# Counting a graph's edges tile by tile in the permuted order: one 128-column product per tile in place of three

## The reference, cut to what matters

```python
for l in range(6):                       # first network, h: [2500, 128]
    W = ssp(edge_attr @ mlp_w1[l] + mlp_b1[l]) @ mlp_w2[l] + mlp_b2[l]
    W = W * C[:, None]                   # cutoff of the edge's length
    msg = (h @ conv_w1[l])[src] * W
    agg = segment_sum(msg, dst)
    h = h + ssp(agg @ conv_w2[l] + conv_b2[l]) @ lin_w[l] + lin_b[l]
x = layernorm(x + h)
for l in range(3):                       # second network, h starts as x
    agg = segment_sum(h[src], dst)
    z = (1 + eps[l]) * h + agg
    h = relu(z @ W1[l] + b1[l]) @ W2[l] + b2[l]
x = layernorm(x + h)
```

## Time and profile before

| | us |
|---|---|
| median of 3 runs | 6492.66 (6480.39 to 6500.86) |
| the profiled execution | 6501.15 |
| its span, first to last instruction | 6499.5 |
| TensorE busy | 5331.1 (82% of the span) |
| GpSimd busy | 4028.7 (62%) |
| VectorE busy | 3774.4 (58%) |
| ScalarE busy | 2761.8 (42%) |
| mean granted TensorE clock | 0.913 of full speed |

### The profile page before, as it was taken

How to read it: one execution, slowest core, us unless ns; L and a number is a source line. 1 busy time by engine, 2 the same in 40 slices (tenths; PEclk the granted TensorE clock), 3 DMA queues, 4 the chain that set the end, 5 groups by cost and what they waited for, 6 DMA issues and landing times.

```text
span 6499.5 us, 130502 instructions
## 1 busy us (share of the span) xinstructions
PE 5331.1 (82%) x34529; PEld 4194.0 (65%) x34530; DVE 3774.4 (58%) x10468; ACT 2761.8 (42%) x4801; POOL 4028.7 (62%) x5030
## 2 busy tenths in 40 slices
PE   1043648999989989989999899998999889998989
PEld 0043637777767777767777677776777767777744
DVE  7321324666666666666666666666666666666632
ACT  0021314445445444445444444444454445444422
POOL 5777762666656666656666566665666656666600
PEclk5576879999999999999999999999999999999999
DMA  8265956333333333233333333333333333333300
GB/s 323 74 222 192 301 173 219 108 106 105 103 103 107 106 105 104 94 112 108 105 106 103 104 106 104 105 101 107 104 108 106 103 99 111 104 106 103 98 15 9
DMA packets 430774, 775.66 MB, mean 119 GB/s; under 512 B 55098, under 2 KB 115972, under 8 KB 427348
## 3 DMA queue, kind: packets, MB, share of 16 engines
q1 hardware_dynamic: 388108, 728.55, 35.0%
q0 software_dynamic: 20640, 34.39, 1.6%
q10 hardware_dynamic: 21928, 11.64, 0.6%
HBM read 605.57 MB, written 168.79 MB: 119 GB/s over the span
## 4 chain that ended last, share of the span: by engine, by line
PE 66%; POOL 9%; issue 9%; DVE 8%; DVEq 5%; DMA 2%; ACT 1%; SPq 1%; ACTq 0%; POOLq 0%
PE ps_a L709 16%; PE ps_h L795 13%; PE ps_a L689 13%; PE ps_w L699 12%; POOL permuted L574 9%; PE ps_pair L721 4%; DVE aggT L1460 3%; PE ps_pair L908 3%; DVE counts L1524 2%; DVEq L341 2%; PE ps_pair L723 1%; DVEq L336 1%; DVEq L430 1%; DVE hid L1599 1%; DMA hid<-permuted 0%
## 5 line engine op out<-in xcount | busy, mean ns | idle before, releaser
L592 POOL TENSOR_SCALAR phot<-pwin_now,prel_now,pcut_now 128x128 f32<-128x128 f32 x4224 | 3315.9, 800 | 1632.9 <-PE ps_a L709 1601.0
L1460 DVE TENSOR_TENSOR aggT<-aggT,ps_a 128x128 f32 x4224 | 1219.0, 289 | 1155.3 <-PE ps_a L709 598.2
L689 PEld LDWEIGHTS ps_a<-hi_mid,buffers 128*128 128x128 f32 x8448 | 1157.6, 199 | 573.0 <-issue 569.8
L1077 ACT ACTIVATE xc<-ps_h 128x512 f32<-128x512 f32 x1056 | 630.3, 597 | 2108.8 <-PE ps_h L795 2093.6
L709 PE MATMUL ps_a<-phot,ex_msg 128*128 128x128 f32 x8448 | 1267.4, 296 | 184.0 <-DVE aggT L1460 183.8
L709 PEld LDWEIGHTS ps_a<-phot,ex_msg 128*128 128x128 f32 x8448 | 1082.8, 201 | 229.8 <-issue 120.5
L795 PE MATMUL ps_h<-buffers,edge_w 112*128 112x512 f32 x2112 | 1181.2, 643 | 11.1 <-DVE hid L1599 9.7
L689 PE MATMUL ps_a<-hi_mid,buffers 128*128 x8448 | 1162.4, 282 | 3.5 <-DMA hi_mid<-node_table 3.5
L699 PE MATMUL ps_w<-edge_w,hid 128*128 128x128 f32 x8448 | 1121.1, 276 | 1.3 <-ACT ps_w L1041 1.1
L1599 DVE SCALAR_TENSOR_TENSOR hid<-xc,ps_h 128x512 f32<-128x512 f32 x1056 | 724.2, 686 | 539.8 <-PE ps_w L699 508.4
L699 PEld LDWEIGHTS ps_w<-edge_w,hid 128*128 128x128 f32 x8448 | 1035.1, 193 | 2.1 <-issue 2.1
(11 more groups left out here) (243 smaller groups left out, 3175.4 us busy)
## 6 DMA issues: line engine op xcount, KB each, us to landing
buffers<-src_select SPq DMA_DIRECT2D x1056, 256.0 KB, 2.7
buffers<-attr_permuted SPq DMA_DIRECT2D x1056, 224.0 KB, 2.8
hid<-permuted SPq DMA_DIRECT2D x176, 208.0 KB, 4.4
counts<-in_rec SPq DMA_DIRECT2D x19, 1404.0 KB, 9.5
permuted<-aggT SPq DMA_DIRECT2D x26, 944.0 KB, 26.6
src_select<-ex_msg SPq DMA_DIRECT2D x88, 256.0 KB
src_select<-buffers SPq DMA_DIRECT2D x88, 256.0 KB
attr_permuted<-ex_msg SPq DMA_DIRECT2D x88, 224.0 KB
```

Source lines behind the costliest of these rows:

```text
L592: op = pool.tensor_scalar(phot[:, u % 2, t, :], pwin_now[:, :], prel_now[:, u * TPG + t:u * TPG + t + 1], pcut_now[:, u * TPG + t:u * TPG ...
L689: mm = pe.matmul(ps_g[:, t * F:(t + 1) * F], select[:, u % AS, t * P:(t + 1) * P], table[:, bass.ds(starts[t], F)], start=True, stop=True)
L1077: act.activation(xc[:, u % 2, :], ps_h[u % 2][:, :], ACT.Exp).then_inc(exp_done, 1)
L1460: dve.tensor_tensor(window, window, ps_a[:, t * PWIN:(t + 1) * PWIN], ALU.add).then_inc(part_added[t] if t < TPG - 1 else add_done[u % M], 1)
```

## The change

Counting takes its tiles from the permuted order, which has 704 tiles (792 with padding that counts nothing). A tile's sources all lie in one block of 125 nodes and its destinations in a window of 128 columns, so one product of a 125-wide source one-hot and a 128-wide destination one-hot, both in 16 bits, gives the tile's whole count. It is added to `counts` tile by tile, at a column worked out from `block_i` and `pbase_i` in registers, from two PSUM buffers taken in turn. `counts` gets 20 slabs of 125 sources with 2,688 columns, and no slab of totals: `sum_counts` makes 20 products for each chunk instead of one. The dense stage turns and multiplies h in blocks of 125 rows. `turn_group` keeps one more column of the records, setup no longer prepares two integer tables of sources but clears some pads, and the semaphores of the counting (and `log_done`) are arranged otherwise. Each of the twelve tiles has a step of its own, 3 to 14.

```diff
-COUNT_STEP = [4, 4, 5, 6, 7, 8, 9, 10, 11, 12, 13, 13]
+COUNT_STEP = list(range(3, 15))
...
-        counts = sb("counts", [P, NB + 1, NCOL], bf16)
+        counts = sb("counts", [P, BLOCKS, NCOL], bf16)
...
                 j, t = q // TPG, q % TPG
                 uses.wait_count(tile_hot[t], j)
-                if t == 0:
-                    uses.wait_count(count_added, j - 1)
-                for first in range(0, NB * WIN, 512):
-                    end = min(first + 512, NB * WIN)
-                    pe.matmul(ps_c[:, first:end], low_hot[:, q % 2, :], pair_hot[:, q % 2, first:end],
-                              start=(t == 0), stop=(t == TPG - 1), skip_group_check=True)
-                pe.matmul(ps_c[t * WIN:(t + 1) * WIN, NB * WIN:(NB + 1) * WIN], ones_mat[:, 0:WIN], dst_hot[:, j % 2, t, :],
-                          start=False, stop=(t == TPG - 1), skip_group_check=True).then_inc(tile_counted[t], 1)
+                uses.wait_count(count_added[(q - 2) % TPG], (q - 2) // TPG)
+                pe.matmul(ps_t[q % 2][:, 0:PWIN], src_hot[:, t, :], dst_hot[:, t, :],
+                          start=True, stop=True).then_inc(tile_counted[t], 1)
...
-                pe.matmul(ps_turn[c % 2][:, 0:nodes_in(c)], ones_mat[:, :], counts[:, NB, c * CH:c * CH + nodes_in(c)],
-                          start=True, stop=True).then_inc(total_summed, 1)
+                for b in range(BLOCKS):
+                    mm = pe.matmul(ps_turn[c % 2][:, 0:nodes_in(c)], ones_mat[:, :], counts[:, b, c * CH:c * CH + nodes_in(c)],
+                                   start=(b == 0), stop=(b == BLOCKS - 1))
+                mm.then_inc(total_summed, 1)
...
-                    mm = pe.matmul(ps_t[c % 2][:, 0:nodes_in(c)], parts[r][:, b * P:(b + 1) * P],
-                                   counts[:, b, c * CH:c * CH + nodes_in(c)], start=first, stop=last)
+                    mm = pe.matmul(ps_t[c % 2][:, 0:nodes_in(c)], parts[r][0:BLK, b * P:(b + 1) * P],
+                                   counts[0:BLK, b, c * CH:c * CH + nodes_in(c)], start=first, stop=last)
...
                 dve.tensor_copy(cut_read[:, g * TPG:(g + 1) * TPG], read_back[:, g % 3, :, COL_CUT])
+                dve.tensor_copy(plocal[:, g * TPG:(g + 1) * TPG], read_back[:, g % 3, :, COL_LOCAL])
...
             def count_slices_now(b, n):
...
+                dve.tensor_copy(rel_count[:, :], prel[:, bass.ds(b * BT, BT)]).then_inc(count_slices, 1)
+                dve.tensor_copy(local_count[:, :], plocal[:, bass.ds(b * BT, BT)]).then_inc(count_slices, 1)
 
             def count_hot(uses, q, n):
...
+                uses.wait_count(tile_counted[q % TPG], q // TPG - 1)
+                dve.tensor_scalar(src_hot[:, q % TPG, 0:BLK], iota[:, 0:BLK], local_count[:, q:q + 1], None, ALU.is_equal)
+                dve.tensor_scalar(dst_hot[:, q % TPG, :], pwin_now[:, :], rel_count[:, q:q + 1], None, ALU.is_equal
+                                  ).then_inc(tile_hot[q % TPG], 1)
+
+            def count_places(j, b):
+                at = b * BT + (j * TPG + PAD)
+                columns = load_starts(mybir.EngineType.DVE, pbase_i, at, START_MAX)
+                blocks = load_starts(mybir.EngineType.DVE, block_i, at, (BLOCKS - 1) * F)
+                return [dve.snap(blocks[t] * (NCOL // F) + columns[t]) for t in range(TPG)]
+
+            def add_count(uses, q, place):
+                window = flat_counts[:, bass.ds(place, PWIN)]
+                uses.wait_count(tile_counted[q % TPG], q // TPG)
+                uses.wait_count(count_added[(q - 1) % TPG], (q - 1) // TPG)
+                dve.tensor_tensor(window, window, ps_t[q % 2][:, 0:PWIN], ALU.add
+                                  ).then_inc(count_added[q % TPG], 1)
...
                             for q in tiles_at(i):
                                 count_hot(uses, q, n)
-                            for q in tiles_at(i - 2):
-                                if q % TPG == TPG - 1:
-                                    add_counts(uses, q // TPG, counted)
+                            for q in tiles_at(i - 1):
+                                if q % TPG == 0:
+                                    places = count_places(q // TPG, counted)
+                                add_count(uses, q, places[q % TPG])
```

More of the change, by code:

```diff
@@ L88 @@
 COUNT_MAX = 255
-LOW = P
 RANK_BLOCKS = 2
@@ L894, in turn @@
                     pe.wait_ge(staged, g * NCH + c - 1)
[L895 to L896 removed]
+                for j in range(PIECE):
+                    mm = pe.matmul(ps_turn[c % 2][:, j * P:(j + 1) * P], hT[:, (c * PIECE + j) * BLK:(c * PIECE + j) * BLK + P],
                                    ident[:, :], start=True, stop=True)
@@ L939, in _ @@
                 with pe.Fori(0, L1) as g:
-                    early, late = range(0, NB - CH // P), range(NB - CH // P, NB)
+                    early, late = range(0, BLOCKS - PIECE), range(BLOCKS - PIECE, BLOCKS)
                     sums(g, 0, 0, early)
@@ L947, in _ @@
                     sums(g, 0, 1, late)
-                    sums(g, 0, 2, range(NB))
+                    sums(g, 0, 2, range(BLOCKS))
                     for c in range(1, NCH + 1):
                         if c < NCH:
-                            sums(g, c, 0, range(NB))
+                            sums(g, c, 0, range(BLOCKS))
                         if c == 1:
@@ L981, in _ @@
             act.sem_inc(picked_done, STEP_PRIME)
-            for s in log_done + seeded:
+            act.sem_inc(log_done, STEP_PRIME)
+            for s in seeded:
                 act.sem_inc(s, PRIME)
@@ L1199, in _ @@
                 dve.sem_inc(s, PRIME)
-            for s in tile_hot + [count_added]:
+            for s in tile_hot + count_added:
                 dve.sem_inc(s, 1)
@@ L1489, in count_slices_now @@
             def count_slices_now(b, n):
-                rel_in, below, inside = (in_window[:, j, :] for j in range(3))
-                dve.tensor_copy(rel_count[:, :], rel[:, bass.ds(b * BT, BT)]).then_inc(count_slices, 1)
-                dve.tensor_copy(low_count[:, :], src_low[:, bass.ds(b * BT, BT)]).then_inc(count_slices, 1)
-                dve.tensor_copy(pair_count[:, :], src_pair[:, bass.ds(b * BT, BT)]).then_inc(count_slices, 1)
-                dve.wait_ge(count_slices, n * 8 + 3)
@@ L1519, in add_counts @@
-            def add_counts(uses, j, b):
-                start = load_start(mybir.EngineType.DVE, base_i, b * BG + (j + LEAD), START_MAX)
-                window = counts[:, :, bass.ds(start, WIN)]
-                uses.wait_count(tile_counted[TPG - 1], j)
-                uses.wait_count(count_added, j - 1)
-                dve.tensor_tensor(window, window, ps_c.rearrange("p (b w) -> p b w", w=WIN), ALU.add
-                                  ).then_inc(count_added, 1)
+                    dve.wait_ge(count_slices, n * 2 + 2)
```

96 lines of the change are left out of this document (36 added, 60 removed).

## The result

The changed kernel takes 5893.68 us (median of four runs, 5888.8 to 5895.9) against 6489.33 for the kernel before (6480.39 to 6500.86): a ratio of 0.908, 95% interval 0.9064 to 0.9096. It is faster by 596 us where 869 were forecast, and the time lies 4 us above the predicted range. The profiled execution has a span of 5894.2 us against 6499.5, so 605 us went.

What follows compares the result with a forecast made beforehand. TensorE was taken to bound the edge loop, with counting on its path. Terms 525 + 271 + 116 - 20 - 20 - 3 = 869 us less gave a forecast of 5625 us, range 5500 to 5890.

Steps and rivals of the forecast that it cites:

- Turn of the iteration: Where iterations meet: VectorE loses a register load, the 672-column add and six slice operations; 116 us gained, between 0 and 187.
- Setup: Setup before the loops: one more copy in 176 groups, mostly covered; 3 us lost, at most 15.
- The wait for the add: Edge loop: TensorE's 132 waits for VectorE's add to counts go, with the slow clock behind; 525 us gained, at least 286.
- TensorE's products: Count steps: one 16-bit product per tile at 0.12 us plus 0.11 for the switch; 271 us gained, between 366 and -15.
- VectorE in a count step: VectorE's work in each count step: 3.45 us, under TensorE's 3.77, so no cost.
- Registers: VectorE's loads and sums once in four tiles: 0.1 us for each of three an iteration, 20 us lost, at most 99.
- First layer norm: 100 products of totals in place of five, all on the path: about 20 us lost, 40 at half clock.
- the register gap: Rival: register work makes VectorE's windows late every four tiles and TensorE waits as before; 768 us more, 6393; 8%.
- VectorE did not become the bound: Rival: VectorE's small operations bound count steps, which stay at 4.13 us; 285 us more, 5910; 17%.
- mutual hold: Rival, slower than before: product and add hold each other, 2.17 us for every tile; 1719 us more, 7344; 3%.
- The clock that does not recover: Rival: TensorE still drops to its lower clock as long as now, for instance at the turn; 239 us stay, 5864; 8%.
- an iteration above 64 us: Sign in the profile after that would make the forecast wrong; the forecast iteration was near 62.4 us.

Runs made afterwards that it cites:

- a_short_back: Changed kernel, waits rearranged (361-instruction VectorE loop), skipped instructions ahead so the loop begins 13 earlier in its piece than the kernel before's: 5864.47 us, ratio 0.8677.
- b_steps: Kernel before with only the steps at which tiles are counted changed, no two fours close together: 5992.95 us against 6472.53.
- a_fit2: Changed kernel with a table of places, fewer waits and a register reused in node steps (349-instruction VectorE loop): 6116.05 us, ratio 0.9077.
- a_fit2_pos: Kernel of a_fit2 with 78 never-executed instructions more ahead of the edge loops: 5800.6 us, ratio 0.8595.
- a_last: Changed kernel with the twelfth tile counted one step earlier, in step 13: 5782.04 us, 112 less than the changed kernel.

## Why the prediction was wrong

The failed step is **Turn of the iteration**: "With that load gone the queue reaches its own work about 0.75 us earlier". It counted which operations of VectorE left the turn and put the branch back at nothing without saying why; in the trace of before it took 0.3 us, in the changed kernel 3.55 in the mean. Together with **Setup**, where the new copy of `turn_group` was priced by its 0.17 us and not as 176 instructions ahead of the loop, it missed that both edits touch where the loop lies and how long it is. Forecast was 1.09 us over plain steps, measured 5.62 in an iteration without node work: 4.53 x 66 = 299 us. Had the code stayed, the term would have come out, the gain even a bit larger than forecast: a_short_back has 0.69. Its second half, the shorter `count_slices_now`, did come out: the step of 4.72 us is a plain one of 3.54 now. What a turn costs too much stands on TensorE as waiting (3.65 us in the turn shown) and as the slow clock behind it (2.04 us for the sums and 1.65 for the next product, in place of 1.13 and 1.02).

The rest, by its terms:

- *The wait for the add*, 525 us: confirmed in kind, 480 by b_steps. The two waiting steps and the two behind them average 7.4 us over plain count steps in each iteration, not the 7.96 of the one wait that I multiplied: 36 us too much.
- *TensorE's products*, 0.23 us a tile taken: 0.11 measured, a gain of 0.12 x 12 x 66 = 95 us over the forecast. The product itself moves the start of the sums by 0.05, less than half of the 0.12 taken from a 32-bit pass; the switch and the rest are the other 0.06.
- *VectorE in a count step*: 3.45 us forecast, 3.30 measured (3.45 from one `hid` to the next below, less a wait of 0.15), under TensorE's 3.65. It still waits for the second product (see `hid` at 2943.55), so it is close to the edge but does not bound the step.
- *Registers*, 0.1 us for each of three taken: 0.35 to 0.38 measured, 51 us too little. TensorE waits 0.17 of it, within the upper bound of 0.5.
- *First layer norm*, 20 us: right. The trace has 98 of the 100 products of totals, in stretches of 8.80, 8.80 and 3.98 us. From TensorE's first product of the norm to VectorE's first pass of it pass 29.15 us, before 9.39: 19.8 us longer.
- *Setup*, 3 us: the loop begins at 1069.0 us in both traces. Nearly right as a time, and the place was not thought of.

VectorE's timeline over a count step without look-ups:

```profile
2940.70 0.26 DVE L1491 TENSOR_SCALAR src_hot<-iota,local_count 128x125 bf16<-128x125 int16 x1
2940.86 0.28 DVE L1492 TENSOR_SCALAR dst_hot<-pwin_now,rel_count 128x128 bf16<-128x128 f32 x1
2941.06 0.28 DVE L1505 TENSOR_TENSOR counts<-counts,ps_pair 128x128 f32 x1
2941.26 1.54 DVE L1452 TENSOR_TENSOR aggT<-aggT,ps_a 128x128 f32 x4
2942.71 0.68 DVE L1459 TENSOR_TENSOR ex_msg<-ps_w,hid 128x512 f32<-128x512 f32 x1
2943.55 0.69 DVE L1581 SCALAR_TENSOR_TENSOR hid<-xc,ps_h 128x512 f32<-128x512 f32 x1 [0.15 <-PE ps_w L696]
```

The sum closes: 299 (turn) + 36 (waits) - 95 (products) + 51 (look-ups) = 291 us more than forecast, against 869 - 605 = 264 in the two profiled executions. The 27 us between are iterations that I had left unchanged and that gained more than the others. The six first iterations of the layers have no branch ahead of them: 71.7 us before and 60.3 now, 2.3 more than the 9.1 of the others. Those with node work went from 79.7 to 70.1, 0.6 more, and the last of a layer 1.2 more. That is 14 + 10 + 6, about 30 us.

Of the rivals, the register gap did not come (0.35 us each, not 3.98), VectorE did not become the bound, and no mutual hold showed. The clock that does not recover came true in a place of its own: not behind the old wait, but behind a new one at the turn. For the same reason the mean clock rose only from 0.913 to 0.920; in b_steps, without the load, it was 0.938. The line that would have shown the forecast wrong, an iteration above 64 us, did.

What the cause is worth: between the first and the last iteration's copy the changed kernel needs 5500.7 - 1069.0 = 4431.7 us, a_short_back 5465.0 - 1327.8 = 4137.2. The difference is 294 us; 5894 less 294 is 5600, 25 us below the forecast. So without the load of code the forecast would have been met, partly by luck: the products gained 95 us more than forecast, the waits and the look-ups 87 less.

The first and the last of these copies in a_short_back:

```profile
L604 POOL COPY prel_now<-prel x66: 236/237/238, 1327.8 to 5465.0; 128x64 f32 x66
```

Open is whether the limit of three pieces holds for other engines' queues, and what exactly the first instructions behind the branch wait for; the traces show the packets and when they move, the gap and the dependence on place, but not which piece is held when. Why three pieces stay and not four is not shown.

## What to carry to other kernels

Count the instructions of a hardware loop on each engine, and where it begins, before an edit is priced: here a loop body that lies within three pieces of 128 instructions, counted from a piece's edge, branches back in 0.3 us, and one that reaches past it took 3.0 to 4.8 us at each turn. TensorE's slow clock can come on top, as behind 58 of 60 turns in the changed kernel. The sign is on the page: megabytes on the instruction queue that grow with the number of turns; the cure can be as small as skipped instructions ahead of the loop (a_fit2's ratio of 0.908 became a_fit2_pos's 0.860). And before a large rewrite, try what its schedule alone would give: one line with the old products gave 480 us, where the whole change gave 596.

## What the runs showed that I had not expected

- **Code is loaded in packets of 8.2 kB** (3.03 MB in 371), five in an iteration, and moving a loop by 128 instructions changed nothing but one packet (64 to 65), while moving it by 64 or by 10 cost 261 and 365 us. The Trainium skill (Runtime: NRT & Kernel Launch, section Instruction fetch mechanics) says that a taken branch whose target has left the window of two pages forces a fetch before execution goes on; the trace agrees in kind, with its 3.7 us. Its page of 16 KiB, 256 instructions, does not agree with the packets and the period of 128 here, and the measurement decides.
- **The place within a piece also sets the price**: the same loop of 355 costs 261 us more when moved by 64 and 365 when moved by 10. Both load five packets in an iteration; the gap at the branch is 3.7 us in the one and 4.4 in the other.
- **TensorE's clock fell behind 58 of the 60 turns with waits of 3.1 to 4.1 us (and behind the 2.17 of the earlier trace rows), and behind 19 of the 60 in a_last, with waits of 1.6 to 2.5 us.** A wait of 1.82 us there was followed by sums of 1.13 us and a first product of 1.02. So a wait that is cut in half can bring back more than its own length. The length alone does not tell: in a_last one of 1.85 us was followed by a step of 5.18 us, and one of 2.16 by a plain one of 3.54.
- **A 128-column product of 16-bit numbers with its load, between 32-bit products, moves what follows by 0.05 us**, where its row gives 0.22 us.
